# Macaron block, FFN 2: the last attention projection spread over four rounds, more moments in the last batch, and the last chunk in row blocks

## The reference, cut to what matters

```
x = x + 0.5 * ffn(layernorm(x))                        # FFN 1
x = x + attn(layernorm(x))                             # attention, 4 heads, causal, output @ Wo * gate
x = x + 0.5 * ffn(layernorm(x))                        # FFN 2
ffn(x):  h = silu(x @ Wg.T / 127) * (x @ Wu.T / 127);  return h @ Wd.T / 127
```

## Time and profile before

| | us |
|---|---|
| median of 3 runs | 491.56 (491.32 to 493.14) |
| profiled execution | 493.74 |
| its span, first to last instruction | 491.9 |
| TensorE busy | 415.6 (84%) |
| ScalarE busy | 386.6 (79%) |
| VectorE busy | 354.5 (72%) |
| GpSimd busy | 266.7 (54%) |

### The profile page before, as it was taken

The page is one execution under the profiler, slowest core; times in us unless marked ns, Lnnn a source line. Parts: engine busy times, 40 slices in busy tenths (PEclk is TensorE's granted clock), DMA queues, the critical chain, the costliest instruction groups (busy, mean ns, idle before and its releaser), DMA issues.

```text
span 491.9 us, 10463 instructions
## 1 busy us (share of the span) xinstructions
PE 415.6 (84%) x3734; PEld 215.1 (44%) x3734; DVE 354.5 (72%) x845; ACT 386.6 (79%) x551; POOL 266.7 (54%) x332
## 2 busy tenths in 40 slices
PE   0558999773767999999999999999999986899995
PEld 0216665452322452543534434534434333566664
DVE  3879796658667786977968869868755809677563
ACT  2588999554567788798897897987986997799952
POOL 3477989843562344534454263453030564799853
PEclk9989999998789999999999999999999999899999
DMA  5267332231420805606205107035070022535542
GB/s 149 65 151 148 71 59 48 47 56 30 100 44 0 172 2 76 98 2 130 43 0 134 37 19 151 2 76 97 1 111 20 7 39 43 85 92 125 128 108 69
DMA packets 119131, 34.89 MB, mean 71 GB/s; under 512 B 101552, under 2 KB 119088, under 8 KB 119088
## 3 DMA queue, kind: packets, MB, share of 16 engines
q1 hardware_dynamic: 118080, 34.15, 34.3%
q10 hardware_dynamic: 1008, 0.20, 0.3%
HBM read 4.98 MB, written 4.19 MB: 19 GB/s over the span
## 4 chain that ended last, share of the span: by engine, by line
PE 46%; DVE 16%; issue 14%; POOL 10%; ACT 9%; DMA 3%; DVEq 1%; POOLq 1%; ACTq 1%; SPq 0%
PE ps L623 10%; PE ps L604 9%; PE ps L628 9%; PE ps L442 7%; DVE H L302 4%; PE ps L490 3%; ACT SG L409 3%; PE ps L481 3%; ACT PT L718 2%; PE ps L512 2%; DVE X L901 2%; POOL HL L367 2%; POOL OL L256 2%; POOL rv L814 2%; PE ps L608 2%
## 5 line engine op out<-in xcount | busy, mean ns | idle before, releaser
L718 ACT ACTIVATE PT<-ps,k_exp 128x1024 f32<-128x1024 f32 (+1 forms) x192 | 162.4, 901 | 22.8 <-PE ps L608 17.7
L442 PE MATMUL ps<-XT,WT 128*128 128x512 f16 x384 | 95.4, 390 | 21.1 <-ACT SG L409 8.4
L604 PE MATMUL ps<-QKT 128*128 128x512 f16 (+3 forms) x384 | 89.0, 334 | 24.5 <-ACT PT L718 13.9
L367 POOL TENSOR_TENSOR HL<-H,HH 128x1024 f16<-128x1024 f32 x32 | 68.4, 2137 | 30.5 <-ACT HH L413 30.4
L623 PE MATMUL ps<-PT,V 128*32 128x512 f32 (+3 forms) x768 | 82.1, 499 | 1.3 <-ACT PVS L752 1.3
L628 PE MATMUL ps<-PT,ones 128*32 128x512 f32 (+3 forms) x768 | 79.9, 487 | 0.0
L302 DVE SCALAR_TENSOR_TENSOR H<-SG,k_isilu,ps 128x1536 f32<-128x1536 f32 x32 | 57.9, 1809 | 14.3 <-ACT SG L409 10.1
L442 PEld LDWEIGHTS ps<-XT,WT 128*128 128x128 f16 x384 | 34.5, 99 | 68.8 <-issue 19.4
L604 PEld LDWEIGHTS ps<-QKT 128*128 128x128 f16 x384 | 28.1, 98 | 81.9 <-ACT PT L718 62.8
L256 POOL TENSOR_TENSOR OL<-ON,OH 128x512 f16<-128x512 f32 x16 | 19.4, 1213 | 80.5 <-ACT OH L252 80.5
L391 ACT ACTIVATE XN<-X,NB,RS 128x128 f32<-128x128 f32 x128 | 52.5, 483 | 4.3 <-POOL NB L345 3.2
(11 more groups left out here) (121 smaller groups left out, 642.6 us busy)
## 6 DMA issues: line engine op xcount, KB each, us to landing
result<-X SPq DMA_DIRECT2D x16, 256.0 KB, 2.5
X<-in_L_attn_x SPq DMA_DIRECT2D x7, 512.0 KB, 4.5
X<-in_L_attn_x SPq DMA_DIRECT2D x2, 256.0 KB, 5.1
XT<-w_int SPq DMA_TRANSPOSE x32, 3.1
AXT<-AS SPq DMA_TRANSPOSE x16, 3.1
QKT<-ST SPq DMA_TRANSPOSE x16, 4.7
w_int<-in_L_ffn_w_gate SPq DMA_DIRECT2D x1, 192.0 KB, 3.8
w_int<-in_L_ffn_w_up SPq DMA_DIRECT2D x1, 192.0 KB, 4.0
```

What stands on the lines that cost most here:

```text
L367: e.tensor_tensor(HL[k % 2][:, :], hidden_16(k), HH[k % 2][:, :], ALU.subtract)\
L442: i = e.matmul(out[:, j, :], WT[:, wp, w * NJ + j, :], XT[k % 2][:, xp, :], start=a == 0, stop=a == len(passes) - 1)
L604: i_ = e.matmul(o, QKT[k % 2][:, i // TPC, NH + hp, i % TPC * P:(i % TPC + 1) * P], QKT[k % 2][:, qc, 2 * hp + h, CH - n:CH], start=True, ...
L718: e.activation(PT[g % 2][:, 2 * hp:2 * hp + 2, 0:n], SCORES[hp][:, :, 0:n], ACT.Exp, scale=k_exp[:, 0:1]).then_inc(a_exp, 1)
```

## The change

1. The last projection is spread: `last_norm` (ON) stands in round 1 behind hidden(1), OH and OL in round 2, the projection on TensorE in round 3, its result in round 4. ON no longer follows the second half of the reciprocal directly.
2. NE is 10: the moments of chunks 6 to 9 are taken in the last batch, too, and rounds -1 to 2 have none. The rstd pairs stay where they were.
3. The last chunk (k = 15 in FFN 2): silu, hidden and down go block by block (three pieces each), all three blocks of down are fp32 products (twelve), and HH and HL are left out. For this WD holds all three blocks.
4. `pv_out` of the last half stands ahead of the `warm` activation.
5. TensorE's loop begins two rounds later (round 5), so that rounds 3 and 4 are written out, in both FFNs.

```diff
-        NE = 6
+        NE = 10
...
-        WD = sb("WD", [P, NW, P])
+        WD = sb("WD", [P, NJ, P])
...
-            first, last = 2 - lo, NC - hi - 2
+            first, last = 3 - lo, NC - hi - 2
...
+        def last_norm(e):
+
+            m = 2 * B - 1
+            e.wait_ge(a_rd, m + 1)
+            e.tensor_tensor(ON[:, :], PVS[:, 0, :], RD[:, :], ALU.mult).then_inc(a_on, 1)
+
...
             i = e.reciprocal(RD[:, cols], PVS[:, 1, cols])
             if half:
                 i.then_inc(a_rd, 1)
-                e.wait_ge(a_rd, m + 1)
-                e.tensor_tensor(ON[:, :], PVS[:, 0, :], RD[:, :], ALU.mult).then_inc(a_on, 1)
...
             def hidden(k, c):
                 g = c + NC * ph
-                e.wait_ge(s_silu, g + 1)
+                if not (ph and k == NC - 1):
+                    e.wait_ge(s_silu, g + 1)
                 e.wait_ge(s_up, g + 1)
                 if k >= 2 or ph:
                     e.wait_ge(s_dn, g - 1)
+                if ph and k == NC - 1:
+                    for j in range(NJ):
+                        e.wait_ge(s_end[0], j + 1)
+                        e.scalar_tensor_tensor(H[k % 2][:, j, :], SG[:, j, :], k_isilu[:, 0:1], U[:, j, :],
+                                               ALU.mult, ALU.mult).then_inc(s_end[1], 1)
+                    return
...
+            def last_on(k, c):
+
+                if ph and k == 1:
+                    last_norm(e)
+
             def last_wo_out(k, c):
 
-                if ph and k == 1:
+                if ph and k == 4:
...
-            pipeline(e, [(0, hidden), (7, stats), (0, last_wo_out), (-1, residual), (7, aggregate)],
+            pipeline(e, [(0, hidden), (0, last_on), (7, stats), (0, last_wo_out), (-1, residual), (7, aggregate)],
...
             def last_o_lo(k, c):
-                if ph and k == 1:
+                if ph and k == 2:
...
-                early = [(rstd_pair, c) for c in range(NE)] + [(x_lo, c) for c in range(3)]
+                early = [(rstd_pair, c) for c in range(6)] + [(x_lo, c) for c in range(3)]
...
+                if ph and k == NC - 1:
+                    for j in range(NJ):
+                        e.activation(SG[:, j, :], G[:, j, :], ACT.Silu, scale=k_silu[:, 0:1])\
+                            .then_inc(s_end[0], 1)
+                    return
...
             def last_o_hi(k, c):
-                if ph and k == 1:
+                if ph and k == 2:
...
             def down(k, c):
                 g = c + NC * ph
-                e.wait_ge(s_h, g + 1)
                 if k >= 1 or ph:
                     e.wait_ge(s_res, g)
+                if ph and k == NC - 1:
+                    for j in range(NJ):
+                        e.wait_ge(s_end[1], j + 1)
+                        for t in range(TPC):
+                            i = e.matmul(DN[:, t, :], H[k % 2][:, j, t * P:(t + 1) * P], WD[:, j, :],
+                                         start=j == 0 and t == 0, stop=j == NJ - 1, skip_group_check=True)
+                    i.then_inc(s_dn, 1)
+                    return
+                e.wait_ge(s_h, g + 1)
...
             def last_wo(k, c):
 
-                if ph and k == 1:
+                if ph and k == 3:
...
             drive(e, step, B, 1, 3)
+            pv_out(B * 2 - 1, B * NG)
             e.activation(warm[:, :], lt_t[:, :], ACT.Silu)
-            pv_out(B * 2 - 1, B * NG)
...
-                e.tensor_tensor(WD[:, :, :], WT[:, 0, 2 * NJ:2 * NJ + NW, :],
-                                WT[:, 1, 2 * NJ:2 * NJ + NW, :], ALU.add).then_inc(s_wd, 1)
+                e.tensor_tensor(WD[:, :, :], WT[:, 0, 2 * NJ:3 * NJ, :], WT[:, 1, 2 * NJ:3 * NJ, :],
+                                ALU.add).then_inc(s_wd, 1)
```

More of the change, by code:

```diff
@@ L167, in macaron_kernel @@
             "full", "free", "cp", "s", "exp", "pv", "pvc", "rd", "on", "oh", "ol", "mx", "last")]
+        s_end = [sem(f"s_end{i}") for i in range(2)]
         d_f, d_x, d_t, d_u = [[sem(f"{n}{i}") for i in range(2)] for n in ("d_f", "d_x", "d_t", "d_u")]
```

## The result

The changed kernel takes 487.57 us (median of 4 runs, 487.48 to 488.82). The kernel before, measured beside it, takes 492.35. The ratio is 0.990 (95% interval 0.986 to 0.994): 1.0% faster. The forecast was 486.1, range 484.6 to 488.2. In the profiled executions 493.74 became 487.54, the span 491.9 became 485.6; the forecast for these was 488.3 and 486.5.

The account below looks back on a forecast made before the run. At FFN 2's entry TensorE waited 4.06 us for the last projection's OL, then ran at slow clock. Entry -5.5, tail 0.0 and down weights +0.1 sum to -5.4: from 491.56 to 486.1 us, range 484.6 to 488.2.

Parts of the forecast that it names:

- The entry: Start of FFN 2, to down(4): spread projection and early moments remove TensorE's wait for OL, 5.5 us saved.
- the walk: Operation-by-operation queue timing of FFN 2's first rounds, using earlier durations: down(4) at 432.4 instead of 437.95, 5.5 us saved.
- cross-check: Same entry saving from pieces: 4.06 waiting, 1.25 projection, about 0.9 slow clock, together 6.2, less 0.67 for the projection elsewhere.
- The cover of the moments: VectorE's 11.02 us idle before the even projection's result hides four chunks' moments; uncovered they would cost 5.0 us.
- the low end of its bounds: ON on VectorE behind hidden(1): forecast to take between 0.69 and 2.14 us.
- The swap of PVS copies and table load: ScalarE before FFN 2: copies ahead of the load, silu(0) 0.3 us later, up(0) loses its 0.69 wait.
- The tail: Last chunk of FFN 2: down(15) still awaits residual(14) behind hidden(15)'s three pieces; 0.0 us, bounds -0.4 and +2.7.
- The down weights: Longer sum on GpSimd at 25.7 us, about 0.9 instead of 0.43: +0.1 us, bounds 0 and 0.5.
- main forecast: Whole kernel's median time as predicted, 485.2 to 487.2 us, chance 0.70.
- the rival with half the shift eaten: Entry of FFN 2: queues without slack, slow ON and late transposes cost 1.5 us, giving 487.6; chance 0.12.
- the clock did not fall at the entry: Rivals: TensorE's clock low at FFN 2's entry for one stretch, 491.3 us, chance 0.07; lasting, 496.4 us, chance 0.03.
- GpSimd's slack: Entry of FFN 2: GpSimd runs without pause, yet h_lo(1) and h_lo(3) come 0.8 to 1.0 us before TensorE wants them.

Follow-up runs that it names:

- wait filled: Kernel before plus 18 idle products on TensorE between down(0) and its wait for OL; 491.24 us, ratio 0.996.
- result late: Changed kernel plus two unused reciprocals on VectorE between the last batch's moments and the even projection's result; 493.12 us, ratio 1.000.
- tail only: Kernel before with only the last chunk changed (three pieces of silu and hidden, twelve fp32 down products, WD whole); 493.09 us, ratio 1.003.
- spread only: Changed kernel with NE = 6 again and the last chunk as before; 489.02 us, ratio 0.993.
- table first: Changed kernel with the silu table loaded ahead of the PVS copies again; 487.16 us, ratio 0.988.

## Why the prediction was right, and where it was not

The entry. Forecast 5.5 us by the walk; down(4), counted from gate(0), moved from 34.34 to 28.81: 5.53. Every station of the walk is in the trace within 0.15 us once it is moved by the 0.56 that gate(0) is earlier: hidden(1) 411.9 forecast, 411.30 + 0.56 measured; down(1) 417.7 and 417.13 + 0.56; down(4) 432.4 and 431.86 + 0.56. The pieces of its cross-check can be told apart by a run: the slow clock was forecast at 1.5 (0.9 on the twelve products, 0.58 on the projection), and "wait filled" measured 1.47 at down(1), 1.23 at the end; the rest was the wait. The 0.9 is 3.65 less the 2.75 that the runs at full clock show; from the 2.89 that the prediction names it would have been 0.76.

The cover of the moments held. Its price was put too low: 5.0 us for 5.0 uncovered counts the wait alone, and "result late" lost 0.8 us more behind a wait of 4.05 because the clock fell (5.35 in all by the medians, 4.5 by the trace).

ON took 0.69, the low end of its bounds. The swap of PVS copies and table load cost silu(0) 0.4, counted from gate(0), for 0.3 forecast; putting it back changes nothing. The load took 1.28 us again. The Trainium skill, "ScalarE: Activation LUTs", section "What ACT_TABLE_LOAD costs", makes its total of about 2.7 us from about 1.28 for the load and about 1.38 for a drain; the load agrees, and the drain doesn't show here, where the load starts 0.03 us after the PVS copies and the next activation 0.01 us after the load.

The tail. Forecast 0.0, measured 0.15. The mechanism was half right: down(15) does wait for residual(14), to 0.1 us as forecast. But the prediction named residual(14)'s place in VectorE's queue as what decides. The run with residual(14) moved forward gives 0.20 of the 1.18 us; what decides is that down(14) and down(15) share one bank, so that a residual must lie between them, wherever it stands. The forecast of 0.0 was right because two limits balance, as its sum says: the HH and HL chain that is gone, and the later start with eight more fp32 products in its place.

The down weights were forecast at +0.1 from 0.9 us of work; they took 0.91, and the early stages vary by more than their effect (see "tail only").

The total. The sum of -5.4 is -5.66 within FFN 2. The trace pair shows 6.3 in the span. 0.56 of it lies ahead of gate(0) and isn't the change's work: it is the difference of two opposite shifts. Attention, from its first QKT product to gate(0), took 278.4 us in the trace before and 276.8 in this one, while FFN 1 came out 1.0 longer here. Over thirteen traces ("result late" with its extra wait left out) attention took 276.8 or 276.9 where the clock over 138.6 to 170 us was 1.00, and 278.2 to 278.4 where it was 0.95. Both kinds occur with the old entry ("tail only" has 1.00, "wait filled" 0.95) and with the new one ("spread only" 1.00, "table first" 0.95). The rows of the kernel before and of the changed one:

```profile
138.60:170.00 31.40, 27.24 (x240) 11.60 (x240) 21.58 (x60) 24.13 (x33) 14.18 (x22) 0.95 0.36 70
...
138.60:170.00 31.40, 25.86 (x240) 11.14 (x240) 22.04 (x65) 25.39 (x35) 14.46 (x22) 1.00 0.38 74
```

The predicted median, 486.1, came out 1.5 low. 0.8 of it is the base: it was counted from 491.56, the median of three runs, and the comparison beside the changed kernel gave 492.35 (11 to 23 runs per chip gave 492.5 to 493.1). The other 0.6 is the difference, 4.8 by the medians of the first comparison for 5.4 forecast; beside the second run of the changed kernel it was 5.35, so the runs don't tell the two apart. The measured 487.57 is therefore outside the 485.2 to 487.2 of the main forecast and at the 487.6 of the rival with half the shift eaten. The trace rules that rival out, since down(4) moved by the full 5.53. That the number fell into the range owes something to luck: the range was drawn wide enough for a rival that did not occur.

The rivals: the clock did not fall at the entry. In "result late", with its pause of 4 us, it did. GpSimd's slack sufficed: no station of the walk came late. The longest transpose between 400 and 450 us landed in 3.6 us.

## What to carry to other kernels

When several engines wait in a ring, look for the one result that stands in everybody's queue too early: giving it more rounds, or taking other work out of its way, buys the same time, so try the cheaper one first and don't add the two. Price a pause of TensorE with the slow clock behind it, 0.8 to 1.2 us on top of 4 here. A finer split of the last piece of work paid here only when the buffer that it writes was free as well: 0.15 us without, 1.3 with it.

## What the runs showed of the hardware

The last store of 256 KB ends 3.1 to 3.5 us after the last residual's end in nine traces and 4.5 to 4.8 in four; the changed kernel has 3.1 in one trace and 4.8 in the other. This spread of the span, up to 1.7 us, has nothing to do with the change.

ON, a product of two SBUF operands, took 2.14 us beside GpSimd's HL (410.35 to 412.47 in "wait filled", ON from 410.88 to 413.02) and 0.69 in the changed kernel, beside GpSimd's power of 128x8 (412.44 to 414.08, ON 413.02 to 413.71). The four traces with ON in the old place have 2.14, the ten with ON behind hidden(1) 0.68 or 0.69. So it is held up by one kind of GpSimd instruction and runs beside another; what sets the two apart is not shown. The Trainium skill, "SBUF — State Buffer", section "SBUF: two separate sides", has the two engines lock a shared pair of ports for the whole instruction in such a case; the first pair of rows agrees, the second doesn't. The rows of "wait filled":

```profile
410.35 2.12 POOL L367 TENSOR_TENSOR HL<-H,HH 128x1024 f16<-128x1024 f32 x1 [1.49 <-ACT HH L413]
...
410.88 2.14 DVE L248 TENSOR_TENSOR ON<-PVS,RD 128x512 f32<-128x512 f32 x1
```

GpSimd's row in the changed kernel's timeline:

```profile
412.44 1.64 POOL L360 TENSOR_TENSOR RS<-RS,nhalf 128x8 f32<-128x8 f32 x1
```
